# Node-feature columns in place of the fourth gather: each sixth group of stage one, split 64 and 64, instead of each eighth, split 8 and 8 per slot

## The reference, cut to what matters

```
msg_in = concatenate([x[src], x[dst], edge_attr], -1)      # 200000 x 384
h = relu(msg_in @ msg_W1 + msg_b1)
messages = h @ msg_W2 + msg_b2
aggregated = segment_sum(messages, dst)
```

## Time and profile before

| what | value |
|---|---|
| median of 3 runs | 4940.12 us (4935.2 to 4942.16) |
| the profiled execution's own time | 4941.37 us |
| its span, first to last instruction | 4938.8 us |
| POOL busy in the span | 2918.5 us, 59% |
| PE busy | 3470.2 us, 70% |
| DVE, ACT busy | 2492.4 us and 2281.2 us, 50% and 46% |
| gathers of stage one | 1517, 954 ns each |

### The profile page before, as it was taken

One profiled execution on the slowest core, in us unless ns is written; L12 is line 12 of the kernel. 1 busy time (PEld: TensorE's weight loads), 2 busy tenths in 40 slices (PEclk: granted clock), 3 DMA queues, 4 the chain that ended last, 5 costly groups with the idle time before them and its releaser, 6 DMA issues.

```text
span 4938.8 us, 90325 instructions
## 1 busy us (share of the span) xinstructions
PE 3470.2 (70%) x21208; PEld 2756.0 (56%) x21208; DVE 2492.4 (50%) x12768; ACT 2281.2 (46%) x8862; POOL 2918.5 (59%) x3098
## 2 busy tenths in 40 slices
PE   4777777777777677767757676666777677676766
PEld 3656655666666555655645555555555555555555
DVE  3344444444444444444435555565555555555555
ACT  3344444444444444444435555555555555555555
POOL 5665656565656565656546556666566656565554
PEclk7677677676776777777678888898888888888888
DMA  5333433343434333333322222222222222222221
GB/s 150 111 111 112 112 110 113 112 112 111 111 111 111 111 111 112 111 112 111 96 67 72 70 71 71 71 72 71 70 71 71 72 71 71 71 71 71 70 71 48
DMA packets 361802, 450.21 MB, mean 91 GB/s; under 512 B 163461, under 2 KB 217827, under 8 KB 361263
## 3 DMA queue, kind: packets, MB, share of 16 engines
q1 hardware_dynamic: 263359, 244.49, 17.2%
q0 software_dynamic: 97504, 199.69, 15.7%
q10 hardware_dynamic: 400, 0.20, 0.0%
HBM read 420.79 MB, written 23.28 MB: 90 GB/s over the span
## 4 chain that ended last, share of the span: by engine, by line
issue 25%; DVE 23%; another core or an unknown queue 20%; PE 17%; ACT 10%; DVEq 3%; ACTq 1%; DMA 0%; SPq 0%
DVE t_logit L2621 3%; PE bank L2475 3%; PE bank L1690 3%; PE bank L2481 3%; DVE lone L911 2%; DVE m_pre L1787 2%; ACT t_z L2552 2%; DVE t_zt L2614 2%; ACT t_a_row L2532 2%; DVE t_chosen L935 1%; PE bank L1678 1%; PE bank L2502 1%; ACT lone L1746 1%; DVEq L907 1%
## 5 line engine op out<-in xcount | busy, mean ns | idle before, releaser
L1014 POOL DMA_INDIRECT t_ring<-tab_l,src_t x1530 | 1447.6, 946 | 999.3 <-issue 351.9
L1014 POOL DMA_INDIRECT m_ring<-tab_a,src_t x1517 | 1446.6, 954 | 971.6 <-issue 388.0
L2475 PE MATMUL bank<-t_ring,t_a_edge 128*128 128x128 f32 x3060 | 537.1, 328 | 728.5 <-ACT t_a_edge L2524 721.2
L2475 PEld LDWEIGHTS bank<-t_ring,t_a_edge 128*128 128x128 f32 x3060 | 450.3, 226 | 782.2 <-ACT t_a_edge L2524 774.4
L1690 PE MATMUL bank<-w,m_attr_t 128*128 128x128 f32 x3128 | 815.1, 390 | 89.6 <-issue 71.7
L1690 PEld LDWEIGHTS bank<-w,m_attr_t 128*128 128x128 f32 x3128 | 695.0, 273 | 175.1 <-issue 126.2
L1787 DVE TENSOR_TENSOR m_pre<-bank,m_ring 128x512 f32<-128x512 f32 (+1 forms) x391 | 264.2, 676 | 1035.3 <-remote 762.2
L2552 ACT ACTIVATE t_z<-bank 128x512 f32<-128x512 f32 x391 | 233.6, 597 | 1034.2 <-remote 536.6
L2614 DVE TENSOR_TENSOR t_zt<-bank,t_z 128x512 f32<-128x512 f32 x391 | 270.5, 692 | 775.5 <-issue 555.1
L1728 ACT ACTIVATE m_hid<-m_pre 128x512 f32<-128x512 f32 x391 | 246.4, 630 | 810.3 <-issue 500.3
L2481 PE MATMUL bank<-t_zt,att_wn 128*128 128x512 f32 x782 | 520.2, 756 | 3.5 <-issue 3.5
(11 more groups left out here) (276 smaller groups left out, 6401.4 us busy)
## 6 DMA issues: line engine op xcount, KB each, us to landing
m_ring<-in_edge_attr_dram SPq DMA_DIRECT2D x390, 256.0 KB
t_rows<-dst_rows SPq DMA_DIRECT2D x196, 256.0 KB
m_rows<-dst_rows SPq DMA_DIRECT2D x196, 192.0 KB
t_ring<-tab_l,src_t POOLq DMA_INDIRECT x1530
m_ring<-tab_a,src_t POOLq DMA_INDIRECT x1517
lone<-tab_l SPq DMA_DIRECT2D x1408, 0.5 KB
m_win<-tab_b SPq DMA_DIRECT2D x391, 24.0 KB
t_win<-tab_r SPq DMA_DIRECT2D x391, 24.0 KB
```

What stands on the lines that cost most here:

```text
L1014: pool.indirect_dma_start(out=r.got[u][0:rows, j, :], out_offset=None, in_=table, in_offset=bass.IndirectOffsetOnAxis(ap=k.src_t[0:rows, g ...
L2475: last = pe.matmul(p_nd[q % 2][:, 3 * W:3 * W + P], lhsT=a_edge[q % 2][:, j, :], rhs=column(k, r, g, j), start=(j == 0), stop=(j == J - 1))
```

## The change

The picked group is one in six (g mod 6 = 5, from group 11 to 389) instead of one in eight (g mod 8 = 7, from 15 to 383): 64 groups, not 47. Its 128 columns are copied in six slots, not eight. Before, a slot copied 8 columns on DVE and 8 on ACT; now DVE has columns 0 to 63 and ACT 64 to 127, and the slot's part is 10 or 11 of each. The fetch of the numbers is in SP's slots with g mod 6 = 3, three slots ahead of the first copy as before.

```diff
-PICKED = P // U
-BY_VECTOR = 8
+PICK = 6
+BY_VECTOR = P // 2
...
 def picked(k, g):
 
-    return g % U == U - 1 and U <= g < k.groups - 1
+    return g % PICK == PICK - 1 and U <= g < k.groups - 1
...
-    n, i = (g + SOONER) // U, (g + SOONER) % U
-    if not many or not picked(k, n * U + U - 1):
+    n, i = (g + SOONER) // PICK, (g + SOONER) % PICK
+    if not picked(k, n * PICK + PICK - 1):
         return
     if i == 0:
         if n == 1:
             eng.wait_ge(k.s_ht, k.n_ht)
         eng.wait_ge(m["m_ids"], 16 * n)
-        after(eng, m["m_hp"], (n - 1) * U if n > 2 else 0)
-    first += i * PICKED
+        after(eng, m["m_hp"], (n - 1) * PICK if n > 2 else 0)
+    first, many = first + many * i // PICK, many * (i + 1) // PICK - many * i // PICK
...
-        after(sp, m["m_picked_v"], U * (n - 2))
-        after(sp, m["m_picked_s"], U * (n - 2))
+        after(sp, m["m_picked_v"], PICK * (n - 2))
+        after(sp, m["m_picked_s"], PICK * (n - 2))
...
-                    if u == 5:
-                        fetch_picked(sp, k, s, t["src"], rnd + 1)
+                    if g % PICK == PICK - 3:
+                        fetch_picked(sp, k, s, t["src"], g // PICK + 1)
...
-                                pe.matmul(p_hid[q % 2][:, e], lhsT=k.lone[:, at[0] % 2, :], rhs=k.w1[:, 0, :],
+                                pe.matmul(p_hid[q % 2][:, e], lhsT=k.lone[:, g // PICK % 2, :], rhs=k.w1[:, 0, :],
...
-                        pick_columns(nc, act, k, s, g, BY_VECTOR, PICKED - BY_VECTOR,
+                        pick_columns(nc, act, k, s, g, BY_VECTOR, P - BY_VECTOR,
```

More of the change, by code:

```diff
@@ L953, in fetch_picked @@
 def fetch_picked(sp, k, m, src, n):
-    g = n * U + U - 1
+    g = n * PICK + PICK - 1
     if not picked(k, g):
@@ L1684, in body @@
                         if picked(k, g):
-                            pe.wait_ge(s["m_picked_v"], g + 1 - U)
-                            pe.wait_ge(s["m_picked_s"], g + 1 - U)
+                            pe.wait_ge(s["m_picked_v"], g + 1 - PICK)
+                            pe.wait_ge(s["m_picked_s"], g + 1 - PICK)
                         for j in range(J):
```

## The result

The changed kernel takes 4956.17 us (median of 6 runs, 4952.04 to 4969.49), the kernel before 4940.6 us (6 runs). The ratio is 1.0035, 95% interval 1.002 to 1.0051: slower by 15.6 us in the medians and some 17 us by the ratio, where I had forecast 13 us faster. The profiled execution took 4952.04 us, its span is 4950.2 us.

The account below looks back on a forecast made before the run. Stage one was taken as bound by POOL's gathers plus one wait a group for PE's results. Terms -18.7 + 2 + 4 = -12.7 us took 4941.4 to 4928.7 us, less 1.3 for the median: 4927 us, range 4904 to 4954 us.

Parts of the forecast that it names:

- the one on the columns: DVE and ACT, stage one: 1088 more copies on each and loads 0.17 us a slot longer, costed at nothing.
- the cover I named: Idle of DVE before m_pre (803.9 us) and ACT before the relu (782.4 us), 2.1 us a group, hiding added copies and loads.
- The pace of stage one, each group its gathers and one wait: POOL in stage one: each group costs its gathers at 1.25 us and one wait of about 1.3 us.
- 17 gathers, 1.1 us each, 18.7 us: POOL in stage one: 17 fewer gathers save 1.1 us each, -18.7 us (range -3.4 to -21.6).
- The 0.2 us of the middle round: Mid stage one: a round with its picked group saved 0.2 us against unpicked groups, the low end per gather.
- rival 4: Stage one: picks leaving the turn of the round shorten waits, 25 us more gained, 4902 us; chance 0.13.
- Gathers beside copies, +4 us: POOL in stage one: gathers slow by 4 ns a copy, so 1088 more copies cost +4 us.
- The single 1.07 us: One stage-one gather beside eight copies took 1.07 us, not 0.94 or 0.95; cited for gathers slowing beside copies.
- rival 2: Stage one: DVE's copies lock out POOL's gathers, +166 us if all falls on them, 5087 us; chance 0.03.
- The last slots, +2 us: End of stage one: copies in slots 385 to 387, after the last gather, 3 x about 0.7 us = +2 us.
- Rival 1: Stage one: added load on DVE and ACT is on the path, +74 us in full, 4995 us, likelier 4950; chance 0.17.
- What would show it: Expected trace signs: 1500 gathers, POOL's waits about unchanged, DVE's idle before m_pre shrinking by about what copies grow.

Follow-up runs that it names:

- e10: Changed kernel with column cuts at multiples of four (0, 12, 20, 32, 44, 52, 64), slower condition: 4911.44 us against 4936.88 for the kernel before, ratio 0.9945.
- e6: Changed kernel with column cuts at multiples of four (0, 12, 20, 32, 44, 52, 64), faster condition: 3887.52 us, ratio 0.994 to the kernel before.
- e3: Changed kernel, but from the third picked group on each slot loads one number and copies one column per engine, faster condition: 3889.18 us, ratio 0.9944.
- e4: Kernel before with 2 or 3 more copies per slot and engine into a spare tile nobody reads, faster condition: 3909.76 us, ratio 0.9997.
- e5: The changed kernel word for word, in the faster condition: 3929.0 us against 3910.36 for the kernel before, ratio 1.0045.
- e12: The changed kernel once more, in the slower condition: 4967.03 us against 4936.88 for the kernel before, ratio 1.0058.
- e7: Kernel before with loads of 11 numbers from three places earlier, eight used, from the second slot on, faster condition: 3911.73 us, ratio 1.0006.
- e9: Kernel before with both misplaced loads of 11 numbers and 10 or 11 copies per slot and engine, slower condition: 4956.82 us against 4936.88, ratio 1.0035.
- e8: Changed kernel with one group in four picked, 16 columns per slot and engine, loads of 16, faster condition: 3847.72 us, ratio 0.9839 to the kernel before.
- e1: Changed kernel with each slot's register load split in two, 8 numbers and 2 or 3, faster condition: 3954.88 us against 3910.31, ratio 1.011.
- e2: Changed kernel with other, uneven column cuts (DVE loads of 8 to 14 numbers, ACT 10 or 11), faster condition: 3956.94 us in one run, beside 3910.31.
- e11: Same kernel as e8, one group in four picked with loads of 16, slower condition: 4929.05 us against 4936.88 for the kernel before, ratio 0.9982.

## Why the prediction was wrong

**The step that failed** is the one on the columns: "8 take 597 ns, 4 take 345 ns, so 63 ns each, 0.17 us more a slot". Both rows were loads from a multiple of four numbers and with a multiple of four to read, and the line through them holds only there. The change's loads are 10 or 11 from places 0, 10, 21, 32, 42 and 53, and took 1.07 us (10 from 0 or 32) or 2.5 us: about 1.4 us a slot more than before on DVE, where I had 0.17. With that the cover I named, 2.1 us a group on DVE, had to hide 1.4 + 0.43 us on average and 2.4 us in four slots of six, and the conclusion "nothing" fell. With the cuts moved to multiples of four and nothing else, the same 64 picked groups gave 0.9945 in the condition of the measurement (e10), and 0.994 in the other (e6). The forecast for the change, 0.9974, was on that side, but it lies outside e10's interval (0.9931 to 0.9959): with the loads put right the gain is 27 us and not 13, so the term of the gathers was mis-sized as well, below.

The Trainium skill (page "Runtime: NRT & Kernel Launch", section "Instruction fetch mechanics") puts a register load, over uncached AXI, at about 200 ns a register even in bulk; these loads read SBUF. An estimate from that page's figure is 2.2 us for 11 numbers. The loads from other places are near it, 2.5 us for 11; those from a multiple of four are not, 0.6 us for 8. I had not weighed it, since the rows of before stood at 75 ns a register.

**Point by point.**
- *The pace of stage one, each group its gathers and one wait*: right for what it was used for. e10 does 312 relus in 1900 us where the kernel before, in the same stretch, did 308. That PE's results come late when gathers run, the trace of the kernel before shows: the semaphore on which m_pre's 162 "remote" waits of 400 to 2300 us end is the one that PE's L1695 raises, and it rises 4.4 us (median) behind the recorded end of L1695; after the last gather it is 14 ns. In the faster condition it is 14 ns throughout, and with aligned loads POOL alone is the bound, at 1.25 us a gather. Why PE is late wasn't tried and stays open.
- *17 gathers, 1.1 us each, 18.7 us*: too small. e10 gained 27 us (interval 20 to 34), 1.6 us for each with the small costs in it, as if the wait shrank in proportion to the gathers; that is argued. In the faster condition e3 and e6 gave 1.25 and 1.35 us. The 0.2 us of the middle round was no guide. That rival 4 (25 us beyond the forecast) named the cause, picks leaving the turn of the round, is not shown; half of its gain would do.
- *Gathers beside copies, +4 us*: not seen. The mean gather was 951 ns in the changed kernel and 954 ns before; in the faster condition it was 950 ns with hardly any copies (e3) and with a third more than before (e4, ratio 0.9997). The single 1.07 us was not a price of copies in general. So rival 2 was not seen in any size with these copies of one element per partition; larger copies no run here tried.
- *The last slots, +2 us*: with aligned loads, from POOL's last gather of stage one to the first of stage two, 38.9 us in e10 against 37.7 us before: +1 us. In the changed kernel it was 42.8 us, +5 us.
- *Rival 1*, load on DVE and ACT, is the side on which it came out, but not by its mechanism: it scaled the shares that the chain of waits gave to copies and loads (+74 us), and a third more copies with fast loads cost nothing in e4 and left e10 its gain. Those shares lay in front of a wait that did not end with them.
- *What would show it*: I said that DVE's idle before m_pre should shrink by about what the copies grow. It shrank by 460 us, and the copies grew by some 180; the missing 280 us and the 530 us before the copies were the sign of a load that I had priced from outside its kind. (The 803.9 us of the earlier trace rows hold only the groups that are gathered whole.) With the picked groups counted in, the idle time before m_pre was 799 us before and 668 us in e10, 400 to 2300 us: 131 us less, for 127 us more of copies, as forecast. In the changed kernel it was 266 us.

**Why it cost 42 to 56 us of a possible 540.** 384 slots with 1.4 us more is 540 us of each of two engines, and the cut alone cost 42 us (e5 against e6) to 56 us (e12 against e10). In the faster condition the idle time before m_pre of groups gathered whole tells how far each kernel is from the edge, 400 to 1800 us (e4, e7, e5):

```profile
L1791 DVE TENSOR_TENSOR m_pre<-bank,m_ring 128x512 f32<-128x512 f32 x252 | 174.3, 692 | 512.3 <-DMA m_ring<-tab_a,src_t 377.8 <-PE bank L1699 134.1
...
L1789 DVE TENSOR_TENSOR m_pre<-bank,m_ring 128x512 f32<-128x512 f32 x251 | 173.5, 691 | 75.5 <-PE bank L1697 74.6 <-issue 0.9
...
L1787 DVE TENSOR_TENSOR m_pre<-bank,m_ring 128x512 f32<-128x512 f32 x237 | 163.9, 691 | 95.9 <-PE bank L1695 94.8 <-issue 0.9
```

In e4 DVE waits for the data of the gathers, so it has time to spare. In e7 that wait is gone, and 288 groups pass in the 1400 us, 4.86 us each: just the pace of its gathers, 3.88 a group at 1.256 us, 4.87 us. The kernel is at the edge and pays nothing. In e5 the wait is gone too, but 283 groups pass, 4.95 us each, where its gathers (3.83 a group) would take 4.81. That is 0.14 us a group too much, and it is paid half along the way and half at the end (e5 against e6: 20.6 us and 19.9 us). DVE's own work with the loads that stick out is 4.5 us a group in both, and not the 5.4 to 5.6 us that e9's expectation gave it; the rest of its time are waits for PE, 107 us in e7 and 127 us in e5. So it is DVE and PE together that pass the edge; which link between them the copies lengthen is not shown. In the slower condition, with 6.2 us a group, nearly all is lost along the way: the last gather of stage one is issued at 2466.79 in the changed kernel and at 2422.78 in e10, and stage two's first comes 42.8 and 38.9 us behind it. There I have the sum of effects (e10, e12, e9) and not the account by slot.

## What to carry to other kernels

A price per item from two sizes holds for their kind alone: write down what else the rows share (here the start and the count were multiples of four) and ask whether the changed code keeps it. When work is cut in unequal parts, choose the cuts for the machine, not for evenness. And where an engine idles before an instruction for "issue", look at its own queue: the time may be a register load, which no busy share counts. For slack, compare the whole slot with the pace, since an addition that is free by itself can use up the slack that the next one needs.

## What the runs showed of the hardware that I had not expected

- A load of registers from SBUF by DVE takes 0.60 us for 8 numbers of four bytes (kernel before), 0.85 us for 12 (e6) and 1.10 us for 16 (e8) when it begins at a multiple of 16 bytes; from any other place 1.9 us for 8 (e1), 2.5 us for 11 (the changed kernel), 3.2 us for 14 (e2). One number takes 0.31 us, whatever the place (e3). ACT's loads take some 5 to 10% less.
- The same program takes 3910 or 4937 us, by the condition. The granted clock in the records differs, 0.884 for e5 and 0.777 for the changed kernel as first measured:

```profile
core 0: 4950.2 us, clock 0.777
```

```profile
core 0: 3931.8 us, clock 0.884
```

  In the slower condition PE's results become visible late while gathers run, 4.4 us (median) and up to 8 us after their recorded end in the waits of m_pre; in the faster one 14 ns after it, and with aligned loads POOL's gaps are the bare 0.30 us. What sets the condition is open. The gain of a change can differ in kind between them (e11: 8 us, e8: 63 us, the same kernel).
